# Keys of a cross-attention made as rows and turned, in place of keys made turned with a product for their sums of squares

## The chip, the cores and the metric

The kernel runs on one core of one Trainium2 chip. The metric is the device time of the whole program in microseconds (us). TensorE is PE in the profile (its weight loads PEld), VectorE DVE, ScalarE ACT, GpSimd POOL, and SyncE, which only issues DMAs here, SP. All matrix work that the change touches is in float32; the records show a float32 matmul as two instructions, a transpose as one.

## The reference, cut to what matters

Four batches of 512 tokens (`x`, 512 wide; a context `ctx`, 256 wide) pass through a state-space layer, a quantized feed-forward, a cross-attention and a mixture of experts. The change lies in the cross-attention's keys alone:

```python
k = (ctx @ Wk).reshape(B, Skv, H, D)      # H = 16 heads of D = 128, Skv = 512
k = k * rsqrt(mean(k * k, axis=-1) + 1e-5) * gk
q = q * rsqrt(mean(q * q, axis=-1) + 1e-5) * gq
scores = einsum("bqhd,bkhd->bhqk", q, k) / sqrt(128)
```

For every token and head the kernel needs k with the 128 of a head on the partitions ("turned", times the gain `gk`), and the sum of squares over those 128, which ends as a scale of the softmax's exponent with one value for a token on a partition.

## The kernel before, in words

All instructions of an engine stand in one fixed order, written out by hand for each engine, with semaphores between them. There is no scheduler.

**Units.** The keys are made in 32 *units*, one for each batch and pair of heads (4 x 8; `GH` = 2 heads, `h` = 0, 1). A unit's turned keys go to DRAM (`kt_dram`) and come back in the attention. 18 units (0 to 17) are made in the *first scan*, the state-space layer of batch 0; unit 18 at its end and beyond. After that comes a *turn* for each batch b = 0 to 3: a *front* (the end of that batch's scan, the feed-forward and, in turns 0 to 2, the start of the next batch's scan) and then the attention's eight *groups*, beside which turns 0 to 2 run the next batch's scan. Turns 0 to 2 make two units each, of which the first begins at the end of the turn before; turn 3 has no scan to run and makes eight, seven of them within its front.

**One unit before.** Line numbers are the profile's; every plain matmul has line 1881, the helper `mm`.
- PE, KT(h), `k_turned`: weights are 128 columns of `wk`, 512 tokens stream past, two matmuls. They fill PSUM bank `pp[h]`.
- ACT, `k_out`: for each h a square of the bank into `k_sq` (L962, 128x512) and a copy times the gain into a staging tile (L967). The latter gives the bank back (`pp_drained`).
- PE, SS(h), `k_sums`: four matmuls, each with 128 columns of squares as weights and one column of ones streaming. The sums come out with tokens on partitions, 4 columns in the same bank.
- ACT, `k_sums_out`: mean plus epsilon into `ssv_k` (L975, 128x4).
- SP, `k_dma`: once KT(1) is in PSUM it loads `wk` for the next unit (L541, at times `ctx_att`, L544), then waits until both banks were given back after the gain copies and stores the staging tile (L557).
- POOL, `key_rms`: a power of -1/2 over many units' columns at once (L771).

**What surrounds it.** The first scan has eight rounds. In each, DVE does `times_b` (L1388), the scans (L1396), `times_c` (L1407) and, in rounds 0 to 5, ternary weights (L1355, L1356); ACT makes the decays (L913), weight sums (L935) and moves turned weights (L944 to L955); PE sums the scan's outputs (`y_sum`, weights `arena` or `xc`) and turns weights. Rounds 0 to 5 carry two units each, rounds 6 and 7 one. PE's order within a round is: KT(0), KT(1) of the first unit, y_sum 0, its SS(0), y_sum 1, its SS(1), KT(0), KT(1) of the second unit, weights, its SS(0), weights, its SS(1). SP's order is: the round's `k_dma`s, then the two broadcast loads `bc` of round r + 2 (L536, into `bc` or `xnT`), which DVE's `times_b` of that round waits for, then a staging load of weights (L573, rounds 0 to 3). Units 16 to 18 follow the last y_sum with little beside them, and after them PE starts batch 1's scan.

In a front, DVE works out quantization scales, ACT rounds turned activations (L1052) and makes the gelus (L1056), and PE alternates between transposes and bf16 matmuls.

Of the kernel before, what the change touches and what calls it, by code (L numbers as in the profile page):

```python
# [15 lines left out]
ALU = mybir.AluOpType  # L16
# [73 lines left out]
K_OFF = {"KT": 0, "SS": 2}  # L90
K_HALF = 2
PP_OFF = {"Q": 0, "QT": 2}
# [3 lines left out]
def program(nc, t):  # L96
    ctx = ExitStack()
    with ctx:
# [84 lines left out]
        k_sq_first = dsum  # L183
# [27 lines left out]
        k_sq_turn = qraw.rearrange("p t w -> p (t w)").rearrange("p (h q) -> p h q", h=GH)  # L211
# [134 lines left out]
        k_squares = sem("k_squares")  # L346
# [160 lines left out]
        def _(sp):  # L507
# [224 lines left out]
        def _(pool):  # L732
# [52 lines left out]
            key_rms(G_FIRST * 2, 0, first_columns(0, 2))  # L785
            def turn(b, off, scan):
# [3 lines left out]
                if b == 0:  # L790
                    key_rms(U_FIRST, 0, first_columns(2, 3))
                rstd(2, 3 * b + 2)
                key_rms(units_after(b), b * NG, turn_columns(b))
# [58 lines left out]
        def _(act):  # L852
# [125 lines left out]
            def first_out(n):  # L978
                k_out(n, 0, k_stage_first[n % 2], k_sq_first if n < U_LATE else k_sq_turn)

            def first_sums_out(n, h):
                k_sums_out(*first_unit(n), 0, h)
# [26 lines left out]
            for n in range(U_EARLY):  # L1009
                first_out(n)  # L1010
                for h in range(GH):
                    first_sums_out(n, h)

            for r in range(TC):
# [3 lines left out]
                first_out(units[0])  # L1018
                for i in range(GH):
                    if r + 1 < TC:  # L1020
                        decay(0, r + 1, i)
                    first_sums_out(units[0], i)
                for n in units[1:]:
                    first_out(n)
                if r + 2 < TC:
                    tern(w_out, r + 2, range(0, 2))
                for n in units[1:]:
                    first_sums_out(n, 0)
                if r + 2 < TC:
                    tern(w_out, r + 2, range(2, 4))  # L1030
                for n in units[1:]:
                    first_sums_out(n, 1)
# [3 lines left out]
            for n in range(U_LATE, U_FIRST):  # L1036
                first_out(n)
                for h in range(GH):
                    first_sums_out(n, h)
            for i in range(GH):  # L1040
                act.wait_ge(hc_done[i], TC + 1)
            k_out(unit_at(0, 0)[0], 0, k_stage_turn[0], k_sq_turn)
            k_sums_out(*unit_at(0, 0), 0, 0)

            def turn(b, off, scan):
# [16 lines left out]
                def kt_out(i):  # L1062
# [1471 lines left out]
```

## Time and profile before

| | us |
|---|---|
| median of 3 runs | 2015.83 |
| lowest, highest | 2007.64, 2020.55 |
| profiled execution, its own time | 2035.78 |
| its span | 2033.8 |
| PE busy | 1876.3 (92%) |
| DVE busy | 1392.9 (68%) |
| ACT busy | 1048.6 (52%) |
| POOL busy | 310.4 (15%) |
| mean granted TensorE clock | 0.961 of 2.4 GHz |

The span runs from the first instruction to the last. A busy share is an average over very different stages, and a busy PE is not a PE at its peak: its matmuls overlap, so that the distance from one start to the next, not a record's length, is what an instruction costs. The same holds for ACT, whose short operations start before the one ahead has ended.

### The profile page before, as it was taken

To read this page: it belongs to the slowest core of one execution; us is meant where nothing else is said; L and a number is where in the kernel's file an instruction comes from. 1 tells how busy PE (TensorE), PEld (TensorE's weight loads), DVE (VectorE), ACT (ScalarE), POOL (GpSimd) and SP (SyncE) were. 2 spreads that over 40 slices of the span, in tenths; PEclk is the share of its full clock that TensorE was granted. 3 is DMA by queue.
4 is the path that set the end of the run, shared out by engine and by line. 5 is a ranking of instruction groups with operands and counts; after the bars stand their busy time and mean duration, and the time that the engine had idled before them with its cause. 6 is when DMAs were issued, how large, how long until landed. Compare 5 with 4: busy or idle time off the path is not lost.

```text
span 2033.8 us, 23853 instructions
## 1 busy us (share of the span) xinstructions
PE 1876.3 (92%) x7070; PEld 1073.2 (53%) x7103; DVE 1392.9 (68%) x1775; ACT 1048.6 (52%) x2256; POOL 310.4 (15%) x189
## 2 busy tenths in 40 slices
PE   6799889899999989999999899998899999998895
PEld 2455444556564455656544556564465656543442
DVE  3699726999997689999956999999254232344422
ACT  4667425755554466556536656563445444443430
POOL 1001210211111011212100212120022111114032
PEclk9799989999999989999999899998899999999997
DMA  5256221222222112222221222222224242302333
GB/s 164 80 165 198 83 88 33 68 83 85 85 82 98 39 47 78 85 84 84 79 73 43 73 78 90 75 93 73 78 99 93 64 90 62 88 30 100 125 108 124
DMA packets 115763, 176.23 MB, mean 87 GB/s; under 512 B 12512, under 2 KB 67552, under 8 KB 115184
## 3 DMA queue, kind: packets, MB, share of 16 engines
q1 hardware_dynamic: 101040, 158.58, 24.1%
q0 software_dynamic: 13840, 15.21, 3.7%
q10 hardware_dynamic: 816, 1.57, 0.2%
q8 instruction: 39, 0.64, 0.1%
q14 instruction: 28, 0.23, 0.0%
HBM read 146.76 MB, written 34.87 MB: 89 GB/s over the span
## 4 chain that ended last, share of the span: by engine, by line
PE 64%; issue 16%; DVE 11%; ACT 4%; POOL 2%; another core or an unknown queue 2%; DMA 1%; DVEq 0%; ACTq 0%; SPq 0%; POOLq 0%
PE ps L1881 21%; PE px L1881 14%; PE pp L1881 14%; PE pd L1881 6%; PE po L1881 5%; DVE arena L1396 3%; PE pp L2226 2%; DVE arena L1388 2%; ACT hbuf L1177 1%; ACT arena L913 1%; DVE arena L1407 1%; DVE arena L1414 1%; DVE arena L1374 0%; DVE arena L1372 0%
## 5 line engine op out<-in xcount | busy, mean ns | idle before, releaser
L1396 DVE TENSOR_TENSOR_SCAN arena<-arena 128x512 f32<-128x512 f32 x256 | 294.3, 1205 | 0.6
L762 POOL TENSOR_TENSOR rms<-ssv,minus_half 128x4 f32<-128x4 f32 x64 | 154.3, 2412 | 795.4 <-ACT ssv L1153 795.4
L1177 ACT ACTIVATE hbuf<-ps,shift,rms_k 128x512 f32<-128x512 f32 x256 | 198.5, 777 | 123.5 <-PE ps L1881 116.0
L1881 PE MATMUL ps<-qkT 128*128 128x512 f32 x512 | 256.0, 612 | 5.6 <-ACT hbuf L1177 3.0
L1881 PE MATMUL pp<-wq,xnT 128*128 128x256 f32 x1024 | 233.4, 382 | 2.9 <-issue 1.5
L1881 PEld LDWEIGHTS pp<-wq,xnT 128*128 128x128 f32 x1024 | 192.1, 190 | 40.7 <-issue 13.4
L1598 DVE SCALAR_TENSOR_TENSOR xc<-px,rden,xc 128x512 f32<-128x512 f32 x192 | 136.2, 740 | 85.0 <-PE px L1881 83.4
L1881 PE MATMUL px<-wo,oT 128*128 128x512 f32 x384 | 183.2, 599 | 0.4
L913 ACT ACTIVATE arena<-arena,a_neg 128x512 f32<-128x512 f32 x256 | 163.3, 710 | 14.4 <-DVE arena L1374 8.4
L1881 PEld LDWEIGHTS ps<-qkT 128*128 128x128 f32 x512 | 91.5, 194 | 132.2 <-ACT hbuf L1177 70.5
L1881 PE MATMUL pp<-ctx_att,wk 128*128 128x512 f32 x256 | 136.1, 676 | 22.5 <-ACT ssv_k L975 6.4
L1881 PE MATMUL po<-hbuf,v_sb 128*128 128x512 f32 x256 | 130.7, 592 | 0.0
L1388 DVE TENSOR_TENSOR arena<-arena,bc 128x2048 f32<-128x2048 f32 x56 | 127.8, 2283 | 0.9 <-DVE v_sb L1356 0.6
L1881 PE MATMUL pd<-hbuf,v_sb 128*128 128x512 f32 x256 | 123.0, 603 | 0.0
L1407 DVE TENSOR_TENSOR arena<-arena,bc 128x2048 f32<-128x2048 f32 x52 | 118.8, 2285 | 0.0
L1881 PE MATMUL ps<-wv,ctx_att 128*128 128x256 f32 x512 | 115.8, 379 | 0.0
L1530 DVE SCALAR_TENSOR_TENSOR hbuf<-px,fsc,ws 128x512 f32<-128x512 f32 x64 | 48.0, 751 | 96.1 <-PE px L1881 93.2
L1414 DVE TENSOR_TENSOR arena<-arena 128x2048 f32<-128x2048 f32 x48 | 112.1, 2335 | 2.3
L1612 DVE TENSOR_TENSOR dsum<-dsum,hbuf 128x512 f32<-128x512 f32 x128 | 88.6, 692 | 29.9 <-ACT hbuf L1177 23.6
L1881 PEld LDWEIGHTS ps<-wv,ctx_att 128*128 128x128 f32 x512 | 97.2, 190 | 13.5
L1881 PEld LDWEIGHTS px<-wo,oT 128*128 128x128 f32 x384 | 69.9, 189 | 58.6 <-issue 39.6
L1161 ACT ACTIVATE qk_raw<-pp,rms 128x128 f32<-128x128 f32 x256 | 72.9, 369 | 48.8 <-POOL rms L762 48.6
(324 smaller groups left out, 2901.7 us busy)
## 6 DMA issues: line engine op xcount, KB each, us to landing
bc<-bc_dram SPq DMA_DIRECT2D x56, 512.0 KB, 4.8
wo<-in_Wo SPq DMA_DIRECT2D x32, 512.0 KB, 3.6
wq<-in_Wq SPq DMA_DIRECT2D x32, 512.0 KB, 3.3
qkT<-kt_dram SPq DMA_DIRECT2D x32, 512.0 KB, 3.5
hbuf<-in_w SPq DMA_DIRECT2D x8, 1024.0 KB, 9.5
wk<-in_Wk SPq DMA_DIRECT2D x32, 256.0 KB, 2.8
wv<-in_Wv SPq DMA_DIRECT2D x32, 256.0 KB, 2.8
kt_dram<-xnT SPq DMA_DIRECT2D x14, 512.0 KB, 3.0
```

Of the source, the lines that this page charges most:

```text
L762: nc.gpsimd.tensor_tensor(rms[:, j], ssv[:, j], half, ALU.pow).then_inc(rms_done, 1)
L913: nc.scalar.activation(dA[i][:, e], delta[:, e], ACT.Exp, scale=a_neg[:, e, bass.ds(g * GH + i, 1)]).then_inc(exp_done[i], 1)
L1161: m = nc.scalar.activation(qraw[:, k, h * D:(h + 1) * D], pp[bank][:, i * GW + h * D:i * GW + (h + 1) * D], ACT.Copy, scale=rms[:, j, h, i ...
L1177: nc.scalar.activation(pT[:, h, k], ps[s_use % 2][:], ACT.Exp, bias=shift[:, 0:1], scale=rms_k[:, bass.ds(G * (GH * NT) + (h * NT + k), 1) ...
L1388: V.tensor_tensor(hb[i], du, bc_i[:, 0:1, :].broadcast_to((P, EC, L)), ALU.mult).then_inc(dbu_done[i], 1)
L1396: V.tensor_tensor_scan(hb[i][:, e], dA[i][:, e], hb[i][:, e], 0.0, ALU.mult, ALU.add).then_inc(scan_done[i], 1)
L1407: V.tensor_tensor(dst, hb[i], bc_i[:, 1:2, :].broadcast_to((P, EC, L)), ALU.mult).then_inc(hc_done[i], 1)
L1414: V.tensor_tensor(u, u, hb[i], ALU.add).then_inc(y_added, 1)
L1530: V.scalar_tensor_tensor(hbuf[:, k % 2, j * 512:(j + 1) * 512], bank, fsc[:, 0, 4, k:k + 1], ws1[:, j * 512:(j + 1) * 512], ALU.mult, ALU. ...
L1598: V.scalar_tensor_tensor(xc[:, k], px[bank][:], rden[:, h, k:k + 1], xc[:, k], ALU.mult, ALU.add).then_inc(px_drained[bank], 1)
L1612: V.tensor_tensor(dsum[:, h], dsum[:, h], pT[:, h, k], ALU.add).then_inc(ds_step[h], 1)
L1881: return nc.tensor.matmul(out, lhsT, rhs, start=first, stop=last, **kw)
```

## The change: what it does

- KT(j) becomes **KR(j)** (`k_rows`): weights are 128 tokens of `ctx_att`, the 256 columns of `wk` (both heads) stream past; four matmuls fill bank `pp[j]` with two blocks of tokens as rows.
- ACT (`k_rows_out`) copies each bank to `k_raw` in SBUF (128x512), waits for this own copy (`k_copied`), then squares the bank in place in PSUM in four pieces of 128x128, each with an accumulated row sum that goes straight to `ssv_k`. The last of the four gives the bank back.
- SS(h) becomes **T(h)** (`k_turned`): four PE transposes of `k_raw`, which wait for both copies. ACT then copies the bank times the gain into the staging tile (`k_turned_out`), where the small L975 stood.
- Mean and epsilon move to POOL, one `tensor_scalar` ahead of each power.
- SP waits for T's copies before it stores the staging tile. The code of `k_dma` is the same, but its second wait now stands for a later event.

```diff
-K_OFF = {"KT": 0, "SS": 2}
+K_OFF = {"KR": 0, "KT": 2}
 K_HALF = 2
+K_COUNTED = GH * NT - 2
...
-        k_sq_first = dsum
+        k_raw_first = dsum[:].rearrange("p h q -> p (h q)").rearrange("p (t w) -> p t w", t=NT)
...
             def k_dma(n, G, groups, stage, g_next, ctx_next=None):
 
-                bank, at_ = k_at(n, groups, "KT", 1)
+                bank, at_ = k_at(n, groups, "KR", 1)
                 sp.wait_ge(pp_full[bank], at_)
...
-            def key_rms(end, groups, cols):
-
-                for h in range(GH):
-                    bank, n = k_at(end - 1, groups, "SS", h)
+            def key_rms(call, end, groups, cols):
+
+                pool.wait_ge(k_squared, end * K_COUNTED)
+                for j in range(2):
+                    bank, n = k_at(end - 1, groups, "KR", j)
                     pool.wait_ge(pp_drained[bank], n + 1)
                 dst, src = cols(rms_k), cols(ssv_k)
+                nc.gpsimd.tensor_scalar(src, src, 1.0 / D, EPS, ALU.mult, ALU.add).then_inc(k_mean, 1)
+                pool.wait_ge(k_mean, call + 1)
...
-            def k_out(n, groups, stage, k_sq):
-
-                for h in range(GH):
-                    bank, at_ = k_at(n, groups, "KT", h)
+            def k_rows_out(n, G, groups, k_raw):
+
+                for j in range(2):
+                    bank, at_ = k_at(n, groups, "KR", j)
                     act.wait_ge(pp_full[bank], at_)
-                    nc.scalar.activation(k_sq[:, h], pp[bank][:], ACT.Square).then_inc(k_squares, 1)
-                    if n == 0:
-                        act.wait_ge(gain_step, 3)
-                    if h == 0 and n >= 2:
-                        act.wait_ge(k_stored[n % 2], n // 2 * 16)
-                    nc.scalar.activation(stage[:, h], pp[bank][:], ACT.Copy, scale=kgain[:, 0:1]).then_inc(pp_drained[bank], 1)
-
-            def k_sums_out(n, G, groups, h):
-
+                    nc.scalar.activation(k_raw[:, 2 * j:2 * j + 2].rearrange("p t w -> p (t w)"), pp[bank][:], ACT.Copy).then_inc(k_copied, 1)
+                    act.wait_ge(k_copied, 2 * n + j + 1)
+                    for i in range(2):
+                        for h in range(GH):
+                            rows = pp[bank][:, i * GW + h * D:i * GW + (h + 1) * D]
+                            col = (G * GH + h) * NT + 2 * j + i
+                            m = nc.scalar.activation(rows, rows, ACT.Square, accum_out=ssv_k[:, col:col + 1])
+                            if i == 1 and h == GH - 1:
+                                m.then_inc(pp_drained[bank], 1)
+                            else:
+                                m.then_inc(k_squared, 1)
+
+            def k_turned_out(n, groups, stage, h):
+
+                bank, at_ = k_at(n, groups, "KT", h)
+                act.wait_ge(pp_full[bank], at_)
                 if n == 0:
-                    act.wait_ge(const_set, 4)
-                bank, at_ = k_at(n, groups, "SS", h)
-                act.wait_ge(pp_full[bank], at_)
-                nc.scalar.activation(ssv_k[:, bass.ds(G * (GH * NT) + h * NT, NT)], pp[bank][:, 0:NT], ACT.Identity, bias=eps[:, 0:1],
-                                     scale=1.0 / D).then_inc(pp_drained[bank], 1)
+                    act.wait_ge(gain_step, 3)
+                if h == 0 and n >= 2:
+                    act.wait_ge(k_stored[n % 2], n // 2 * 16)
+                nc.scalar.activation(stage[:, h], pp[bank][:], ACT.Copy, scale=kgain[:, 0:1]).then_inc(pp_drained[bank], 1)
...
-            def k_turned(n, groups, loads, h):
+            def k_rows(n, groups, loads, j):
 
                 pe.wait_ge(ctx_att_in, loads * 16)
                 pe.wait_ge(wk_in, n * 16 + 16)
+                bank, at_ = k_at(n, groups, "KR", j)
+                pe.wait_ge(pp_drained[bank], at_)
+                for i in range(2):
+                    k = 2 * j + i
+                    for c in range(CC):
+                        m = mm(pp[bank][:, i * GW:(i + 1) * GW], ctx_att[:, c, k * P:(k + 1) * P], wk[:, c], c == 0, c == CC - 1)
+                m.then_inc(pp_full[bank], 1)
+
+            def k_turned(n, groups, k_raw, h):
+
                 bank, at_ = k_at(n, groups, "KT", h)
                 pe.wait_ge(pp_drained[bank], at_)
-                for c in range(CC):
-                    m = mm(pp[bank][:], wk[:, c, h * D:(h + 1) * D], ctx_att[:, c], c == 0, c == CC - 1)
-                m.then_inc(pp_full[bank], 1)
-
-            def k_sums(n, groups, k_sq, h):
-
-                bank, at_ = k_at(n, groups, "SS", h)
-                pe.wait_ge(pp_drained[bank], at_)
-                pe.wait_ge(k_squares, n * GH + h + 1)
+                pe.wait_ge(k_copied, n * 2 + 2)
                 for k in range(NT):
-                    m = mm(pp[bank][:, k:k + 1], k_sq[:, h, k * P:(k + 1) * P], ones[:, 0:1], True, True)
+                    m = nc.tensor.transpose(pp[bank][:, k * P:(k + 1) * P], k_raw[:, k, h * D:(h + 1) * D], ident[:])
                 m.then_inc(pp_full[bank], 1)
```

Every call of the old functions is replaced in place: `first_out` by `first_rows_out`, `first_sums` and `kss` by `first_turned` and `ktt`, `kt` by `krr`, and so on. The engines' orders of calls are the same.

ACT in round 3 of the first scan, from the decays on (`arena<-arena,a_neg`). `pp` are the banks, `dsum` holds the squares before and the rows after, `wo` and `wq` are the staging tiles, `ws` and `w2t` receive turned weights. Before:

```order
L913 ACTIVATE arena<-arena,a_neg 128x512 x4
L975 ACTIVATE ssv_k<-pp,eps 128x4
L962 ACTIVATE dsum<-pp 128x512
L967 ACTIVATE wq<-pp,kgain 128x512
L962 ACTIVATE dsum<-pp 128x512
L967 ACTIVATE wq<-pp,kgain 128x512
L946 ACTIVATE ws<-px 128x128
L955 ACTIVATE w2t<-px 128x4x128 x2
L975 ACTIVATE ssv_k<-pp,eps 128x4
L955 ACTIVATE w2t<-px 128x4x128 x2
L975 ACTIVATE ssv_k<-pp,eps 128x4
```

And now:

```order
L919 ACTIVATE arena<-arena,a_neg 128x512 x4
L988 ACTIVATE wo<-pp,kgain 128x512
L968 ACTIVATE dsum<-pp 128x512
L974 ACTIVATE pp,ssv_k<-pp 128x128 x4
L968 ACTIVATE dsum<-pp 128x512
L974 ACTIVATE pp,ssv_k<-pp 128x128 x4
L952 ACTIVATE ws<-px 128x128
L961 ACTIVATE w2t<-px 128x4x128 x2
L988 ACTIVATE wq<-pp,kgain 128x512
L961 ACTIVATE w2t<-px 128x4x128 x2
L988 ACTIVATE wq<-pp,kgain 128x512
```

The staging tile is now written where the small operations stood, the second half of it as the last ACT work of the round.

PE in the same round, y_sum 0's end to the second unit, before:

```order
L1881 MATMUL pd<-xc,ident 128x512
L1881 MATMUL pp<-ones,dsum 128x1 x4
L1881 MATMUL ps<-arena,ident 128x512 x2
L1881 MATMUL po<-arena,ident 128x512
L1881 MATMUL pd<-arena,ident 128x512
L1881 MATMUL pp<-ones,dsum 128x1 x4
L1881 MATMUL pp<-ctx_att,wk 128x512 x4
```

And now:

```order
L1893 MATMUL pd<-xc,ident 128x512
L2000 MATMUL pp<-ident,dsum 128x128 x4
L1893 MATMUL ps<-arena,ident 128x512 x2
L1893 MATMUL po<-arena,ident 128x512
L1893 MATMUL pd<-arena,ident 128x512
L2000 MATMUL pp<-ident,dsum 128x128 x4
L1893 MATMUL pp<-wk,ctx_att 128x256 x8
```

Each four matmuls of one column became four transposes, and four matmuls of 512 columns became eight of 256.

## Rows read from the trace of the kernel before

**Rows 1.** Busy time by stretch: round 4, then stretches named in the text.

```profile
core 0: us, PE busy (x) PEld busy (x) DVE busy (x) ACT busy (x) POOL busy (x), PEclk, DMA share, GB/s
161.00:182.00 21.00, 20.12 (x103) 12.00 (x103) 20.65 (x17) 15.40 (x29) 0.00 (x0) 1.00 0.65 197
245.00:292.00 47.00, 40.14 (x131) 22.46 (x130) 8.07 (x18) 13.20 (x27) 0.95 (x1) 0.82 0.29 97
669.00:743.00 74.00, 70.45 (x301) 36.39 (x305) 48.23 (x82) 39.48 (x46) 3.87 (x2) 0.96 0.14 46
1412.00:1518.00 106.00, 88.35 (x406) 52.57 (x409) 50.33 (x94) 43.38 (x73) 6.27 (x3) 0.92 0.25 92
```

**Rows 2.** Chain that ended last, shares of the span, from the page.

```profile
PE 64%; issue 16%; DVE 11%; ACT 4%; POOL 2%; another core or an unknown queue 2%; DMA 1%; DVEq 0%; ACTq 0%; SPq 0%; POOLq 0%
```

**Rows 3.** Timeline of DVE, rounds 4 to 7: start, length, what, idle before.

```profile
161.50 2.29 DVE L1388 TENSOR_TENSOR arena<-arena,bc 128x2048 f32<-128x2048 f32 x1 [0.21 <-DVE v_sb L1356]
...
182.57 2.29 DVE L1388 TENSOR_TENSOR arena<-arena,xnT 128x2048 f32<-128x2048 f32 x1 [0.21 <-DVE qkT L1356]
...
221.73 2.28 DVE L1388 TENSOR_TENSOR arena<-arena,xnT 128x2048 f32<-128x2048 f32 x1
```

**Rows 4.** Timeline of ACT, a unit and its small operations.

```profile
170.12 0.60 ACT L962 ACTIVATE dsum<-pp 128x512 f32<-128x512 f32 x1 [0.54 <-PE pp L1881]
170.61 0.68 ACT L967 ACTIVATE wq<-pp,kgain 128x512 f32<-128x512 f32 x1
171.18 0.28 ACT L946 ACTIVATE ws<-px 128x128 f32<-128x128 f32 x1
...
174.77 0.26 ACT L975 ACTIVATE ssv_k<-pp,eps 128x4 f32<-128x4 f32 x1 [0.20 <-PE pp L1881]
...
179.37 2.55 ACT L913 ACTIVATE arena<-arena,a_neg 128x512 f32<-128x512 f32 x4
```

**Rows 5.** Chain in order of time: start, length, what.

```profile
402.59 3.45 PE pp L1881 x16
...
1423.80 2.80 DMA wk<-in_Wk
...
1443.15 0.60 ACT dsum L962
...
1450.88 3.43 PE pp L1881 x8
...
1467.61 0.87 PE ps L2074 x8
...
1493.96 0.80 PE pp L1881 x8
```

**Rows 6.** ACT, a query's squares with row sums: timeline, then all 256.

```profile
435.03 0.28 ACT L1148 ACTIVATE qk_raw<-pp 128x128 f32<-128x128 f32 x1 [0.39 <-PE pp L1881]
...
436.20 0.30 ACT L1153 ACTIVATE ssv<-ss,eps 128x4 f32<-128x4 f32 x1
...
L1148 ACT ACTIVATE qk_raw<-pp x256: 254/278/322, 372.4 to 1762.2; 128x128 f32<-128x128 f32 x128
L1148 ACT ACTIVATION_READ_ACCUMULATOR qk_raw<-pp x256: 189/212/257, 372.6 to 1762.3; 128x1 f32 x128
```

**Rows 7.** Issues of SP in round 5; then landings of L536 there.

```profile
213.61 1.30 SPq L536 DMA_DIRECT2D xnT<-bc_dram  x2
...
DMA to landing us min/median/max: 6.6/7.0/7.4
```

**Rows 8.** Issues of SP in rounds 2 and 3; then landings of L536 in 3.

```profile
151.49 1.30 SPq L536 DMA_DIRECT2D bc<-bc_dram  x2
...
171.38 0.36 SPq L557 DMA_DIRECT2D kt_dram<-wq  x1
...
DMA to landing us min/median/max: 6.5/8.0/9.4
```

**Rows 9.** Timeline of POOL, first group of turn 3.

```profile
1513.71 10.52 POOL L771 TENSOR_TENSOR rms_k<-ssv_k,minus_half 128x64 f32<-128x64 f32 x1
```

More of the change, by code:

```diff
@@ L345, in program @@
         k_stored = [sem("k_stored0"), sem("k_stored1")]
-        k_squares = sem("k_squares")
+        k_copied = sem("k_copied")
+        k_squared = sem("k_squared")
+        k_mean = sem("k_mean")
         v_full = [sem("v_full0"), sem("v_full1")]
@@ L984, in ctx_load, with first_turned_out @@
+            def first_turned_out(n, h):
+                k_turned_out(n, 0, k_stage_first[n % 2], h)
             def ctx_load(s):
@@ L1017, in _ @@
                     tern(w_sums, r + 2)
-                first_out(units[0])
+                first_rows_out(units[0])
                 for i in range(GH):
@@ L1021, in _ @@
                         decay(0, r + 1, i)
-                    first_sums_out(units[0], i)
+                    first_turned_out(units[0], i)
                 for n in units[1:]:
-                    first_out(n)
+                    first_rows_out(n)
                 if r + 2 < TC:
@@ L1060, in hq_out, with krr_out, ktt_out @@
                         rounded(("F2T", k), j, hqT[:, k % 2, 4 * j:4 * j + 4, :])
-                def kt_out(i):
-                    k_out(unit_at(b, i)[0], b * NG, k_stage_turn[i % 2], k_sq_turn if scan else k_sq_first)
-                def kss_out(i, h):
-                    k_sums_out(*unit_at(b, i), b * NG, h)
+                def krr_out(i):
+                    k_rows_out(*unit_at(b, i), b * NG, k_raw_turn if scan else k_raw_first)
+                def ktt_out(i, h):
+                    k_turned_out(unit_at(b, i)[0], b * NG, k_stage_turn[i % 2], h)
                 if scan:
                     scan_a(b + 1, turn_, 0)
-                    kss_out(0, 1)
+                    ktt_out(0, 1)
                     scan_a(b + 1, turn_, 1)
-                    kt_out(1)
+                    krr_out(1)
                     scan_silu(b + 1, turn_, range(0, 2))
-                    kss_out(1, 0)
+                    ktt_out(1, 0)
                     scan_silu(b + 1, turn_, range(2, 3))
-                    kss_out(1, 1)
+                    ktt_out(1, 1)
                 else:
-                    kss_out(0, 1)
+                    ktt_out(0, 1)
                     for i in range(1, 4):
-                        kt_out(i)
-                        kss_out(i, 0)
+                        krr_out(i)
+                        ktt_out(i, 0)
                         if i < 3:
-                            kss_out(i, 1)
+                            ktt_out(i, 1)
                 for k in range(NT):
@@ L1113, in turn @@
                 if not scan:
-                    kss_out(6, 0)
-                    kss_out(6, 1)
-                    kt_out(7)
+                    ktt_out(6, 0)
+                    ktt_out(6, 1)
+                    krr_out(7)
                 if scan:
@@ L2022, in _ @@
                 y_sum(r, 0)
-                first_sums(units[0], 0)
+                first_turned(units[0], 0)
                 y_sum(r, 1)
-                first_sums(units[0], 1)
+                first_turned(units[0], 1)
                 for n in units[1:]:
@@ L2039, in _ @@
                 if n > U_LATE:
-                    first_sums(n - 1, 1)
+                    first_turned(n - 1, 1)
                 first_k(n, 1)
-                first_sums(n, 0)
+                first_turned(n, 0)
             n0 = unit_at(0, 0)[0]
-            k_turned(n0, 0, B, 0)
-            first_sums(U_FIRST - 1, 1)
-            k_turned(n0, 0, B, 1)
-            k_sums(n0, 0, k_sq_turn, 0)
+            k_rows(n0, 0, B, 0)
+            first_turned(U_FIRST - 1, 1)
+            k_rows(n0, 0, B, 1)
+            k_turned(n0, 0, k_raw_turn, 0)
             def turn(b, off, scan):
@@ L2101, in ffn1_with_turned, with krr, ktt @@
                     ffn1(k, range(2, 4))
-                def kt(i, h):
-                    k_turned(unit_at(b, i)[0], b * NG, b + B, h)
-                def kss(i, h):
-                    k_sums(unit_at(b, i)[0], b * NG, k_sq_turn if scan or i == 0 else k_sq_first, h)
+                def krr(i, h):
+                    k_rows(unit_at(b, i)[0], b * NG, b + B, h)
+                def ktt(i, h):
+                    k_turned(unit_at(b, i)[0], b * NG, k_raw_turn if scan or i == 0 else k_raw_first, h)
                 for i in range(2):
@@ L2143, in turn @@
                 else:
-                    kss(4, 0)
-                    kt(5, 0)
-                    kss(4, 1)
-                    kt(5, 1)
+                    ktt(4, 0)
+                    krr(5, 0)
+                    ktt(4, 1)
+                    krr(5, 1)
                 ffn1_with_turned(2, 0)
                 if not scan:
-                    kss(5, 0)
+                    ktt(5, 0)
                 ffn2(0, 0, 4)
@@ L2154, in turn @@
                 else:
-                    kss(5, 1)
+                    ktt(5, 1)
                 ffn1_with_turned(3, 1)
                 if not scan:
-                    kt(6, 0)
-                    kt(6, 1)
+                    krr(6, 0)
+                    krr(6, 1)
                 ffn2_with_turned(1)
                 if not scan:
-                    kss(6, 0)
-                    kt(7, 0)
-                    kss(6, 1)
-                    kt(7, 1)
+                    ktt(6, 0)
+                    krr(7, 0)
+                    ktt(6, 1)
+                    krr(7, 1)
                 ffn2_with_turned(2)
                 if not scan:
-                    kss(7, 0)
+                    ktt(7, 0)
                 ffn2(3, 0, 4)
                 if not scan:
-                    kss(7, 1)
+                    ktt(7, 1)
                 def xn_turned():
```

100 lines of the change are left out of this document (49 added, 51 removed).

## The prediction

> **What bounds the kernel now.** I read first the chain that ended last: PE stands for 64% of the span, DVE for 11%, ACT for 4% [rows 2]. So a microsecond of ACT is mostly free and one of PE mostly not. An average decides nothing here, though, and the busy time by stretch [rows 1] shows four different situations for the units:
> - In a round of the first scan DVE is busy 20.65 of 21.00 us, PE 20.12 and ACT 15.40. DVE's rounds start at 161.50 and 182.57, 21.07 apart, with 0.21 idle between, spent on DVE's own previous instruction [rows 3]. DVE sets the pace, PE is just under it, and ACT has some 5.7 us to spare. 16 of the 32 units lie here.
> - In 245 to 292 (units 16 to 18) DVE is busy 8.07 of 47 us and ACT 13.20: PE and its loads are the path.
> - In the front of turn 1 (669 to 743) PE is busy 70.45 of 74 us. The fronts of turns 0 to 2 carry two units each.
> - In the front of turn 3 (1412 to 1518), with seven units, PE is busy 88.35 of 106 us, DVE 50.33, ACT 43.38: a ring in which each waits for the others in turn.
>
> **PE's part.** KT was four matmuls of 512 columns for a unit, each recorded as two: 8 records took 3.43 us [rows 5]. KR is eight of 256 columns, 16 records, and the query's 16 records of that shape took 3.45 us [rows 5]. Same price; the doubled weight loads hide behind columns, as they do for the query. SS(h) was 8 records in 0.80 us; T(h) is four transposes, and 8 transposes took 0.87 us [rows 5], so 0.43. Each of the 64 calls saves 0.37 us, 23.7 us of PE time in all. That is the most that the change could bring by work removed.
>
> **ACT's part.** Before, a unit cost for each h a square of 0.49 us and a copy of 0.57 from start to start (170.12, 170.61, 171.18 [rows 4]) and an L975 of 0.16 (its record is 0.26 long, but the next instruction started 0.16 later, counted from the same overlap as those), together 2.44. Now, for each j: a copy that has to end before the squares start, so its 0.60 record and no overlap, say 0.65; then four squares with row sums. The trace has these, into SBUF: four took from 435.03 to 436.20, where the dependent L1153 started, 1.17 with the end of the last; from start to start I take 0.25 each, 1.0 [rows 6]. Then 0.57 for each gain copy. A unit costs 2 x (0.65 + 1.0) + 2 x 0.57 = 4.44, 2.0 more, 64 us over all units. In place in PSUM no row shows a square. It can hardly cost less than 0.22, and not more than its two records end to end, 0.278 + 0.212 = 0.49 [rows 6]. I take 0.25, the row of the same operation, and keep 0.49 for a rival.
>
> Against the change speaks the fixed part of an instruction, paid eight times instead of twice. The row gives 8 x 0.25 = 2.0 us for what 2 x 0.49 did. The Trainium skill (ScalarE: Activation LUTs, "What ACT_TABLE_LOAD costs") puts an ACTIVATE with immediate operands at 186 ns plus 0.833 a column, with 93 ns of overlap. By that, an estimate, eight pieces cost 1.6 us and ACT's extra would be 1.6 us a unit instead of 2.0. The same page says that writing PSUM is faster for ScalarE than writing SBUF ("Step-by-step: what each stage is for"); no row here shows such a write.
>
> **Where it lands.** *First scan.* ACT gets 2 x 2.0 = 4.0 us more in a round and has 5.7. The decays for the next round, at 179.37 [rows 4], start about 1.2 us later, with some four to spare before DVE's scans, since DVE first has a 2.3 us product after 182.57 [rows 3]. PE gives back 4 x 0.37 = 1.5 us a round. All of this is covered by DVE: worth 0. If the cover went, ACT would set the pace; that is a rival.
>
> But SP is moved. Its store of the staging tile at 171.38 [rows 8] followed the second gain copy at once. Now this copy stands where ACT's last L975 of the round stood, at 174.77 [rows 4], which I estimate to end at 174.6 (PE arrives about 1 us earlier, ACT has 0.6 more per bank, and the copy itself takes 0.6). The store and everything behind it on SP slip by 3.2 us, and right behind it stand the two `bc` loads for DVE's round after next. In round 5 these are issued at 213.61 and the first lands 6.6 later, at 220.2 [rows 7]; DVE needs it at 221.73 [rows 3]. Slack 1.5, slip 3.2: DVE stalls 1.7 us. In round 2 they are issued at 151.49 and land first at about 158.0 by round 3's 6.5 [rows 8], needed at 161.50 [rows 3]: with 3.2 more, just in time. In round 3 they follow the store at 171.38 by less than 1 us and land first near 178.7, needed at 182.57 [rows 3], slack near 4: hidden. I take **+2** for the scan; bounds 0 and, were every one of six rounds 1.5 short, +9.
>
> *Units 15 to 18.* Eight T calls on PE's path save 3.0. Each unit's second KR waits for a 0.6 us gain copy instead of a 0.16 to 0.27 operation, three times +0.4, and T of unit 18 waits 0.65 for the second row copy, with nothing left beside it. **-1**.
>
> *Fronts 0 to 2.* Three T calls each, 1.1 us, less 0.4 for the gain copy that now stands ahead of the rounding of activations: -0.7 each, **-2**.
>
> *Front of turn 3.* The cycle over `wk` is unchanged (2.80 us [rows 5]). After unit 3's second bank ACT needed square, gain copy and L975 before it could round activations; the chain runs through it (1443.15 [rows 5]). Now it is copy, squares and a gain copy, +1.05 us; again, 0.65 each, after units 5 and 6. The T calls give 14 x 0.37 = 5.2, of which I count half where PE is on the path: net **0**. POOL's power of 64 columns took 10.52 us [rows 9] and the group's first use follows on it. The new `tensor_scalar` before it is bounded by 0 and, from the power's fit of 0.16 a column, 10.5; since it is multiply and add, I take 0.7, of which 0.5 is covered by ACT's own work: **+0.2**, with a further microsecond in the range. Its sister calls come where POOL is nearly idle (busy 3.87 of 74 us in a front, 0.00 of 21 in a round [rows 1]): 0.
>
> **Sum:** 2 - 1 - 2 + 0 + 0.2 = -0.8 us against the profiled 2035.78, that is 2035.0. The profiled execution stands 20 us above the median of 2015.83, so the forecast for the median is 2015.0. About 1% (20 us) is what can be told from no change.
>
> **Rivals.**
> 1. *PE's saving comes through.* For it: PE 92% busy, and the chain's 64% [rows 2]. Against: half the T calls lie under DVE's 21.07 us rounds. Outside there are 32, 11.8 us; with none of the ACT delays this is 2004. To pass 1% it needs all 64 or a better granted clock besides (it is 0.82 in 245 to 292 [rows 1]; at most 0.18 x 47 = 8 us are to be had there). That gives 1995. Chance 0.10.
> 2. *ACT becomes the bound of the first scan (slower).* If a square in PSUM costs its full 0.49, a unit costs 2 x (0.65 + 1.96) + 1.14 = 6.4, 3.9 more; a round then holds 15.40 + 7.8 = 23.2 us of ACT work against 21.07. It decides from 0.36 a square on (5.7 us to spare, 16 squares a round). Price: 2.1 x 6 rounds = 13, SP's slip doubled in two rounds 4, three waits of 1 us in turn 3's front plus one in each of units 16 to 18, 6: +23, 2039. For it: the squares are now in the ring between bank and PE; against: the same instruction into SBUF overlaps [rows 6]. Chance 0.12.
> 3. *SP's slip grows.* The 1 MB staging load of weights behind `bc` in rounds 0 to 3 pushes the `wk` load of the next unit, PE comes late to the sums of the scan, and each round loses 1.5 us: +9 to +14, 2027. Seen in DVE waiting for DMA. Chance 0.10, within 1%.
> 4. *It does not do what it says*: KR's weight loads do not hide. SS, which is little but weight loads, takes 0.10 us a record [rows 5]; 8 more in each of 16 units outside the rounds are +13, 2029. The query's row speaks against it [rows 5]. Chance 0.02.
>
> **The numbers.** Forecast within 10 us of 2015: 0.66. The forecast and rivals 3 and 4 are "same", 0.78, less what of rival 3 exceeds 20 us: 0.76. Faster by over 1%: 0.11. Slower by over 1%: rival 2 and a little of what no case names, 0.13. The range from 2001 to 2032 leaves out rival 2, most of rival 1's far end and some of the spread of the runs themselves (13 us between lowest and highest).
>
> **What would show it.** T(h) 8 transposes in 0.87 us; KR 3.45 for 16. Squares in `pp` 0.25 apart and ACT busy about 64 us more, less where records overlap. DVE rounds still 21.07 apart, except that the product that starts round 7 waits for a DMA (1 to 3 us). ACT busy 19 to 20 us of a round. The fronts of turns 0 to 2 shorter by under 1 us, that of turn 3 within 2. Wrong would be it if DVE waits for ACT's decays or PE's sums in the scan, if rounds stretch beyond 21.5, or if a front moves by more than 3 us.

## The result, and the profile after

The changed kernel takes 2032.76 us (median of 4 runs, 2031.59 to 2033.83) beside 2015.6 for the kernel before (4 runs): ratio 1.0088, 95% interval 1.0059 to 1.0117, that is 12 to 24 us slower. Forecast were 2015.0, which is no change that could be told, and a range up to 2032. The median lies 0.8 us above that range.

The two profiled executions, 2035.78 before and 2033.81 after, must not be subtracted. Near the end the one of before has a stall that the other lacks: the timelines of ACT, first of before, then of after, at the same instruction.

```profile
2006.64 0.60 ACT L1265 ACTIVATE oT<-px 128x512 f32<-128x512 f32 x1 [30.18 <-remote]
```

```profile
2004.52 0.60 ACT L1277 ACTIVATE oT<-px 128x512 f32<-128x512 f32 x1 [8.00 <-PE px L1893]
```

It goes with the chip, not with the kernel. The part behind the last turn took 179 to 182 us in the four traces of the runs e5 to e8, all from one chip, and 196 to 204 in the eight of the other runs, from three others, with kernels of both sorts in each group; in the two executions compared here it took 201.8 and 178.6. The kernel before had medians of 2015.6 to 2036.9 on the chips used. So below there are ratios to runs on the same chip, and times of stages within a trace. By stage, from the starts of POOL's marks (L746, L756 and L771 before, L749, L759 and L777 after) that end them:

| Stage | before | after | after, second trace |
|---|---|---|---|
| first scan, to 239.94 before | 239.94 | 259.11 | 260.72 |
| units 16 to 18 | 52.08 | 51.05 | 49.47 |
| front of turn 0 | 90.23 | 92.25 | 92.25 |
| attention of turn 0 | 261.08 | 261.44 | 261.41 |
| front, attention of turn 1 | 117.26, 261.41 | 116.63, 262.92 | 116.63, 262.93 |
| front, attention of turn 2 | 117.40, 277.06 | 119.22, 277.46 | 119.22, 277.45 |
| front of turn 3 | 111.46 | 109.22 | 109.27 |
| attention of turn 3 | 304.13 | 303.93 | 304.41 |

The loss is in the first scan, 19.2 and 20.8 us; the other stages together add 2.0 and 0.9 us (forecast: -2.8). The rounds of DVE in the scan, in the timeline of after (the first line of each):

```profile
119.48 2.29 DVE L1400 TENSOR_TENSOR arena<-arena,bc 128x2048 f32<-128x2048 f32 x1 [0.21 <-DVE v_sb L1368]
...
144.61 2.29 DVE L1400 TENSOR_TENSOR arena<-arena,xnT 128x2048 f32<-128x2048 f32 x1 [2.27 <-DMA xnT<-bc_dram]
...
170.42 2.29 DVE L1400 TENSOR_TENSOR arena<-arena,bc 128x2048 f32<-128x2048 f32 x1 [1.94 <-DMA bc<-bc_dram]
...
195.34 2.29 DVE L1400 TENSOR_TENSOR arena<-arena,xnT 128x2048 f32<-128x2048 f32 x1 [1.94 <-DMA xnT<-bc_dram]
...
221.18 2.29 DVE L1400 TENSOR_TENSOR arena<-arena,bc 128x2048 f32<-128x2048 f32 x1 [1.88 <-DMA bc<-bc_dram]
...
240.89 2.29 DVE L1400 TENSOR_TENSOR arena<-arena,xnT 128x2048 f32<-128x2048 f32 x1 [1.64 <-DMA xnT<-bc_dram]
```

Where they were 21.07 apart [rows 3], they are 25.13, 25.81, 24.92 and 25.84, and DVE waits for `bc`. These four lose 17.3 us; the next, 19.71 for 17.99, loses 1.7. But that wait of 2 us is the end of the story, not its cause. The chain of waits in one round of after:

```profile
146.61 0.86 PE pd L1893 x2
147.46 0.44 PE pp L2000 x4
147.90 4.19 issue
152.09 6.13 PE pp L1893 x16
158.23 0.02 issue
158.25 0.61 ACT dsum L968
158.86 0.02 issue
158.88 1.21 ACT pp L974 x8
...
162.71 3.46 PE pp L1893 x16
```

PE is through with all that it has at 147.90 and stands still for 4.19 us. The profile names nothing for this ("issue"); what starts at 152.09 is KR of the round's second unit, which needs `wk`. SP's issues of after, from the store of one round to the `wk` load of the next, and then how long the `wk` load of 140.19 was under way; then the same of the load of 158.03 before:

```profile
137.62 0.36 SPq L560 DMA_DIRECT2D kt_dram<-wq  x1
138.02 1.31 SPq L539 DMA_DIRECT2D xnT<-bc_dram  x2
139.38 0.51 SPq L576 DMA_DIRECT2D hbuf<-in_w  x1
140.19 1.48 SPq L544 DMA_DIRECT2D wk<-in_Wk  x1
...
163.77 0.36 SPq L560 DMA_DIRECT2D kt_dram<-wq  x1
164.17 1.31 SPq L539 DMA_DIRECT2D bc<-bc_dram  x2
165.52 0.51 SPq L576 DMA_DIRECT2D hbuf<-in_w  x1
166.19 1.57 SPq L544 DMA_DIRECT2D wk<-in_Wk  x1
...
DMA to landing us min/median/max: 11.8/11.8/11.8
```

```profile
158.03 0.37 SPq L541 DMA_DIRECT2D wk<-in_Wk  x1
...
DMA to landing us min/median/max: 7.7/7.7/7.7
```

140.19 + 11.8 is 152.0, to 0.1 us when PE goes on. With nothing ahead of it this load takes 2.8 us. Before, 6.5 us lay between `bc` (151.49 [rows 8]) and the `wk` load behind it (158.03); now 2.2 (138.02 to 140.19): the 1 MB of `bc` and the 1 MB staging load have moved back with the store, `wk` of the next unit has not. It is released by the keys of the next round's first unit, which PE had done at 140.16 (136.44, 3.72 long).

And the delay closes a ring, from one issue of `wk` to the next, by two paths of nearly the same length. By SP: landing 11.8, KR 6.1, ACT, the transposes and the gain copy up to the store 5.6, `bc` and staging load on SP 2.4, together 25.9 us. By PE: landing 11.8, KR 6.1, sign matmuls and transposes, with a wait for ACT between, 4.3, KR of the next round's first unit 3.6, together 25.8. The issues are 26.0 apart (140.19, 166.19). SP was through with the staging load at 166.03; the keys it waits for were complete at 166.17 (the last line of the chain above). So the path by PE ended last, by 0.1 us.

The granted clock adds to it. Busy times of after in the two stretches:

```profile
core 0: us, PE busy (x) PEld busy (x) DVE busy (x) ACT busy (x) POOL busy (x), PEclk, DMA share, GB/s
147.80:152.00 4.20, 0.10 (x1) 0.00 (x0) 4.20 (x5) 1.14 (x2) 0.00 (x0) 0.78 0.72 288
152.09:158.20 6.11, 6.11 (x18) 4.93 (x19) 6.08 (x5) 1.81 (x9) 0.00 (x0) 0.60 0.04 15
```

The DMA engines move 288 GB/s while PE waits, 15 GB/s after. The granted clock is 0.60 of full speed over the 6 us right behind PE's idle time, most of them thus at 1.2 of its two levels 1.2 and 2.4 GHz, and the 16 records of KR take 6.12 us there, 3.62 where PE had not waited: 2.5 us more. The four waits took 4.92, 4.19, 4.08 and 3.72 us, the four KRs behind them 1.7, 2.5, 1.5 and 2.9 more than 3.62.

The rest of the profile after. ACT's timeline in a unit, the squares' group, and a group of transposes:

```profile
139.30 0.62 ACT L968 ACTIVATE dsum<-pp 128x512 f32<-128x512 f32 x1
139.96 0.26 ACT L974 ACTIVATE pp<-pp 128x128 f32<-128x128 f32 x1
140.13 0.19 ACT L974 ACTIVATION_READ_ACCUMULATOR pp<-pp 128x1 f32 x1
140.22 0.27 ACT L974 ACTIVATE pp<-pp 128x128 f32<-128x128 f32 x1
...
141.07 0.58 ACT L968 ACTIVATE dsum<-pp 128x512 f32<-128x512 f32 x1
...
L974 ACT ACTIVATE pp<-pp x256: 260/265/271, 72.3 to 1523.6; 128x128 f32<-128x128 f32 x128
L974 ACT ACTIVATION_READ_ACCUMULATOR pp<-pp x256: 182/186/196, 72.5 to 1523.8; 128x1 f32 x128
L2000 PE MATMUL pp<-ident,dsum x184: 272/273/421, 74.2 to 1531.3; 128*128 128x128 f32 x184
```

A copy with its wait 0.66, four squares from 139.96 to 141.07, 0.28 each [rows 4, 6]. POOL's new operation, and the power [rows 9]:

```profile
1535.09 0.24 POOL L774 TENSOR_SCALAR ssv_k<-ssv_k 128x64 f32<-128x64 f32 x1
1535.42 10.52 POOL L777 TENSOR_TENSOR rms_k<-ssv_k,minus_half 128x64 f32<-128x64 f32 x1
```

### The profile page after: what moved, and what is told of

Same layout as the page of the kernel before. It is cut to its first block, busy times and chain, and to the rows that moved or that the text cites. A ratio compares the mean times of both kernels' runs of the same rounds, so it can differ in the third digit from the quotient of the medians.

```text
span 2031.8 us, 24337 instructions
## 1 busy us (share of the span) xinstructions
PE 1860.1 (92%) x7070; PEld 1095.2 (54%) x7103; DVE 1392.6 (69%) x1775; ACT 1109.9 (55%) x2704; POOL 313.2 (15%) x195
## 4 chain that ended last, share of the span: by engine, by line
PE 68%; issue 20%; ACT 5%; DVE 5%; POOL 2%; DMA 1%; SPq 0%; ACTq 0%; DVEq 0%; POOLq 0%
PE ps L1893 22%; PE pp L1893 15%; PE px L1893 14%; PE pd L1893 7%; PE po L1893 6%; PE pp L2240 1%; ACT hbuf L1189 1%; ACT arena L919 1%; ACT pp L974 1%; PE pp L2000 1%; DVE arena L1426 1%; DVE ln_st L1429 0%; POOL ln_r L759 0%; DVE xc L1610 0%; POOL rms_k L777 0%
## 5 line engine op out<-in xcount | busy, mean ns | idle before, releaser
L1893 PE MATMUL pp<-wk,ctx_att 128*128 128x256 f32 x512 | 138.1, 427 | 41.0 <-issue 21.8
L1893 PEld LDWEIGHTS pp<-wk,ctx_att 128*128 128x128 f32 x512 | 107.4, 216 | 63.8 <-issue 43.9
```

The source lines that it names most:

```text
L1893: return nc.tensor.matmul(out, lhsT, rhs, start=first, stop=last, **kw)
```

## The experiments

Theory A: the slip of SP's store puts `bc` and staging load right ahead of the next unit's `wk` load, PE waits for `wk`, and the ring becomes slower than DVE. Theory B: ACT's additional work between KR and the transposes stretches the rounds.

**The slip undone (e1_store_last).** In the changed kernel:

```
-                for n in round_units(r):
-                    first_dma(n)
-                (bc loads, staging load)
+                for n in units:
+                    first_dma(n, loads if n == units[-1] else None)
     (k_dma: wk load, then loads() if given, then the wait for the gain copies, then the store)
```

> The changed kernel; in the first scan SP issues the bc loads and the weight staging load before it waits for the round's last gain copy and stores the key tile, so these loads stand again about 1.3 us behind the wk load, as before the change. Nothing else moves. Theory A (SP's order: the wk load of the next unit stands behind 1 MB of bc and 1 MB of staging load, lands 12 us after its issue and holds PE, ACT and again SP): rounds of DVE go back from 25.1 to 25.8 us to 21.0 to 21.5, the scan is 17 to 20 us shorter, median 2014 (2009 to 2018). Theory B (ACT's 2 us more for each unit, between KR and the transposes, stretch the ring): rounds stay at 24 to 26, median 2028 to 2033.

Measured: ratio 0.9982 (0.9968 to 0.9997). DVE's rounds are 21.06, 21.07, 21.07, 21.17 and 17.99 long, the scan ends at 240.14. ACT does all of its additional work in it. A holds; B, as the cause of the loss, falls. Where the ring is slower than DVE, ACT's squares do lie in it (the 1.21 us of the chain above); at DVE's pace they cost the scan nothing.

**The slip alone in the kernel before (e2_before_slip).**

```
-                    bank, at_ = k_at(n, groups, "KT", h)
+                    bank, at_ = k_at(n, groups, "SS", h)     # first scan only
                     sp.wait_ge(pp_drained[bank], at_ + 1)
```

> The kernel before; only SP's store of a unit's key tile in the first scan waits for the L975s of the unit too, so that the store and all behind it are issued some 3 us later, as in the changed kernel. PE and ACT do what they did. Theory A: the slip alone is enough, rounds of 24 to 26 us where there were 21.07, 12 to 19 us longer, median 2030 (2026 to 2035). Theory B: without ACT's extra work the slip costs only what DVE waits for bc in round 7, 1.7 us: 2015 to 2019.

Measured: 1.0087 (1.0058 to 1.0116), the changed kernel's own ratio. Rounds of 24.82, 24.07, 25.81, 25.04 and 22.01 us. From DVE's round 1 to the end of the scan it takes 19.4 us more than before; the changed kernel 19.1 and, in its second trace, 20.5. Neither PE nor ACT does anything new here: one wait on SP is enough for the whole loss. PE waits 2.64 to 3.57 us four times, with KT at 5.06 to 6.52 us behind it for 3.68. SP was through with the staging load at 134.99 and issued `wk` at 135.92, when PE had done KT of the first unit (132.21, 3.68 long): the ring by PE alone.

**A smaller staging load (e3_small_stage, e10_half_stage).**

```
-                    w_stage(r + 4, r % 2, 2)
+                    w_stage_part(r + 4, r % 2)     # columns 0:256 (e3), 0:1024 (e10)
```

> The changed kernel; in rounds 0 to 3 of the first scan the staging load brings 256 of the 2048 columns (128 KB of 1 MB), so that the quantized weights of the last part are made of old columns. Theory A: 0.9 MB less stands ahead of the wk load, which lands 3 to 5 us earlier; PE no longer waits (3.7 to 4.9 us in each of four rounds) and its keys run at the full clock; rounds 0 to 3 shrink to 21 to 23 us, 10 to 16 us in all, median 2020 (2016 to 2025). Theory B: no change, 2031 to 2034.

> The changed kernel; in rounds 0 to 3 the staging load brings 1024 of the 2048 columns (512 KB of 1 MB), the others stay old. At the 197 GB/s of a round, 0.5 MB are 2.7 us. The changed kernel's ring is 25 to 26 us; less 2.7, and less the 2.5 us that KR loses at the lower granted clock if PE waits less, 20 to 23 us: about DVE's 21.07. So most of the loss is gone with half of the bytes, ratio 0.998 to 1.003. Were the loss in proportion to the bytes, half of it: 1.003 to 1.006.

Measured: with 128 KB 0.9997 (0.9976 to 1.0017), better than the 2020 expected: rounds of 21.07, `wk` lands after 7.5 to 8.0 us. In round 7 DVE waits 1.05 us for `bc`, all that is left of the slip. With 512 KB 1.0038 (1.0023 to 1.0052), outside the 0.998 to 1.003 expected and within what was named for a loss in proportion to the bytes: the rounds take 22.21, 23.03 and 23.70, `wk` lands after 9.4 to 11.1. The ring's 25.9 minus 2.7 us is 23.2, about what they reach; that is still over DVE's 21.07, and each of the three rounds pays the difference. PE on e10, at KR behind its wait:

```profile
144.46 5.24 PE L1897 MATMUL pp<-wk,ctx_att 128*128 128x256 f32 x16 [2.55 <-issue]
```

Two of its four waits, 2.55 and 2.38 us, still have KR at the lower clock behind them (5.24 and 5.38); behind those of 3.23 and 1.77 it takes 3.69.

**The loads between the units (e4_loads_between).**

```
+                first_dma(units[0])
+                loads()                  # bc and staging load
+                for n in units[1:]: first_dma(n)
```

> The changed kernel; in the first scan the bc loads and the staging load are issued between the two units of a round, some 10 us earlier than in the kernel before, and stand ahead of the wk load for the next round's first unit in place of its second. Theory A: DVE never waits for bc; rounds 21.0 to 21.5, median 2012 to 2016, unless the wk load for the first unit becomes late in turn (issued after KR of the second unit, needed about 8 us later, 12 us if it lands as late as now): then 1 to 4 us for each of four rounds, 2018 to 2028. Theory B: 2028 to 2033.

Measured: 1.0216 (1.0189 to 1.0242), the worst of all. The rounds are 26.31, 30.19, 28.23, 30.20 and 24.46 us. The 8 us of slack that I expected aren't there: behind KR of the second unit PE has only two groups of sign matmuls and a few transposes before KR of the next round's first unit, some 4 us, and now that unit's `wk` had the 2 MB ahead of it. PE stands still for 7.55, 8.12, 7.11, 8.24 and 6.25 us; the second and the last of these end with the context's load, which is issued behind `wk`:

```profile
194.12 8.24 issue
202.37 6.10 PE pp L1897 x16
```

The second unit's `wk` has the sums of the scan to hide behind, 8 us. So of the places tried for the whole 2 MB on SP's queue only one costs nothing: right behind the `wk` load for a round's first unit, where the kernel before has it.

**The staging load on ScalarE's queue (e5_stage_act).**

```
-                    sp.wait_ge(stage_used[r % 2], r // 2 + 2)      # SP
-                    w_stage(r + 4, r % 2, 2)
+                    act.wait_ge(stage_used[r % 2], r // 2 + 2)     # ACT, end of its round
+                    act.dma_start(stage[r % 2]..., src).then_inc(stage_in[r % 2], 16)
```

> The changed kernel; the staging load of rounds 0 to 3 is issued from ScalarE's queue at the end of ScalarE's round, no longer from SP's. The bytes are the same, only they don't stand in SP's queue ahead of the wk load. If the order in one queue is what delays wk (theory A1), this is worth what leaving the bytes out was: wk lands after 8 us at most, rounds of 21.07, ratio to the kernel before 0.997 to 1.002. If the 16 DMA engines themselves are the limit (theory A2), wk's packets share with the 1 MB all the same and land 10 to 12 us after issue: rounds of 24 to 26, ratio 1.005 to 1.009.

Measured: 0.9969 (0.9955 to 0.9983), the best ratio of a kernel that leaves nothing out. `wk` lands after 8.2 to 9.7 us, the rounds are 21.8, then 21.06. But ACT issued the load at 129.24, 1.4 us ahead of `bc` (130.65), where SP would have issued it 1.4 behind: the run mixes another queue with a head start, and so does not tell A1 from A2. The Trainium skill (DMA: Bandwidth & Descriptors, "Issuing engines are not separate DMA queues") says that all queues run on the same 16 DMA engines and that starting DMAs from several engines only saves the time of issuing. No run here measures the throughput that this is about.

The next run keeps the queue and changes the order alone.

**The staging load behind `wk` (e11_stage_behind_wk).** Same queue, same bytes:

```
-  store, bc, staging load | wk (next round's k_dma)
+  store, bc | wk, staging load
```

> The changed kernel; SP issues the staging load of a round directly behind the next wk load (that of the second unit) in place of directly ahead of it, some 1 to 2 us later than now. Same bytes, same queue, store and bc where the change has put them. In e5_stage_act the load was also issued 2.7 us earlier than by SP, so that run does not separate the order from the head start; this one does. If what counts is what stands ahead of wk: wk lands 8 to 9 us after issue, rounds of 21.07 to 21.8, scan 17 to 19 us shorter, ratio 0.996 to 1.001. If the engines carry all that is under way side by side, wk lands 11 to 12 us after issue as now: ratio 1.006 to 1.010.

Measured: 1.0007 (0.9996 to 1.0019). SP and PE in it:

```profile
135.02 0.37 SPq L544 DMA_DIRECT2D wk<-in_Wk  x1
135.43 1.86 SPq L578 DMA_DIRECT2D hbuf<-in_w  x1
```

```profile
144.38 3.69 PE L1896 MATMUL pp<-wk,ctx_att 128*128 128x256 f32 x16 [1.05 <-issue]
```

The store and `bc` slip as in the changed kernel, the load is even issued later, and the loss is gone: `wk` lands after 9.3 us (8.9 to 9.4 in the four rounds), PE waits 1.05 and KR takes 3.69. The rounds are 21.06 to 21.19, and only round 7 waits for `bc`, 1.20 us.

What is issued behind `wk` is not free either. In the next round of this trace there is no staging load, `wk` (197.97) is issued 2.2 us after `bc` (195.73), 2.0 in the rounds with one, and it lands after 6.9 us. So, by these rows, the 1 MB costs `wk` 2.4 us when issued 0.4 us behind it and 4.9 when issued ahead of it (11.8 in the changed kernel).

**What ACT's squares cost (e6_one_square, e7_squares_sbuf).** Both from e1_store_last:

```
-                    for i in range(2):
-                        for h in range(GH):
+                    for i in range(1, 2):                  # e6: the last square of four
+                        for h in range(GH - 1, GH):
```

```
-   activation(k_raw[...], pp[bank], ACT.Copy).then_inc(k_copied, 1)
+   activation(k_raw[...], pp[bank], ACT.Copy).then_inc(pp_drained[bank], 1)      # e7
-   activation(rows, rows, ACT.Square, accum_out=...)       # rows in pp
+   activation(k_junk[...], rows, ACT.Square, accum_out=...) # rows in k_raw
```

> The version that stores last (e1_store_last), with one square of 128 columns for each row bank in place of four: six of eight squares with row sums of each unit are left out (the sums of the other rows are a constant). ACT loses 1.7 us a unit. In the scan nothing may change (DVE sets its pace). If ACT's squares lie on the path outside the scan as the prediction counted them (0.4 for a wait in units 16 to 18 and in fronts 0 to 2, 1.05 + 2 x 0.65 in the front of turn 3): 3 to 7 us less than e1_store_last, ratio 0.995 to 0.997. If they are covered everywhere: the same as it, 0.998.

> The version that stores last, with the squares read from the SBUF copy of the rows and written to SBUF of their own: the copy alone frees the PSUM bank, and the transposes wait for the two copies, not for the squares. ACT does as much. If the squares between copy and freed bank cost time outside the scan: 1 to 4 us less than e1_store_last, ratio 0.996 to 0.9975. If not, 0.998 as e1_store_last.

Measured: e6 0.9964 (0.9951 to 0.9976), e7 0.9978 (0.9967 to 0.9988), beside 0.9982 for e1. Six of eight squares left out in 32 units are worth some 4 us at most, and the intervals overlap; taking the squares out of the bank's way is worth nothing that can be told. The front of turn 3 took 110.69 us in e6 and 112.50 in e7, at a granted clock of 0.94, and 109.18 in e1, at 0.97. The changed kernel's own code took 112.03 at 0.94 in e5 (see the fronts below), so the 2 to 3 us expected can't be read from this stage.

**Controls.** The kernel before with e1's order:

> The kernel before with SP's order of e1_store_last (loads ahead of the wait for the round's last gain copy and the store). Control: whether e1_store_last's small gain over the kernel before comes from the order. In the kernel before the store waited only 0.9 us, so the loads move by about 1 us: ratio 0.999 to 1.001. If the order itself brought the gain: 0.998.

Measured 0.9997 (0.9984 to 1.0010): the order brings nothing of its own. All three edits together:

> Three of the edits together: stores last (e1_store_last), the staging load on ScalarE's queue (e5_stage_act), squares from the SBUF copy (e7_squares_sbuf). The scan is already at DVE's pace in each of them, so they should not add up: ratio 0.996 to 0.998. If each gain were of its own, 0.993 to 0.995.

Measured 0.9983 (0.9975 to 0.9992): they do not add up. The changed kernel again:

> The changed kernel once more, beside the others on one chip. Ratio 1.006 to 1.012 as measured. Its second trace tells which stage differences come back: the scan 19 us longer, units 16 to 18 and the front of turn 3 shorter by 1 and 2 us, the front of turn 2 longer by 2 us. What does not come back within 0.5 us is the spread of one execution.

Measured 1.0090 (1.0070 to 1.0110); its stages stand in the table above. From the turns on they come back within 0.5 us. The scan does not, 1.6 us longer, and units 16 to 18 are 1.6 shorter; both together end at 310.16 and 310.19. That the turns come back does not make their differences the kernel's: e5, with the same code in them, has other fronts (see below).

So the change with SP's order mended is 0.2 to 0.3% faster than the kernel before (e1, e5, e7, e9: 0.9969 to 0.9983, each interval below 1), 3 to 6 us. e11, in which PE still waits 0.6 to 1.6 us a round, isn't (1.0007).

## Why the prediction was wrong

**The step that failed is the scan's term, +2 us with bounds 0 and +9.** It measured 19.2. The slip itself was right: forecast 3.2, measured 3.4 (the first round's store went from 107.75 to 111.15). What I then asked was only who needs `bc` and when. That answer was nearly right too: DVE stalls in round 7 for 1.7 us by the forecast, for 1.05, 1.50 and 1.20 us in e3, e5 and e11, where PE is not held up. I did not ask, in the sum, what comes behind the moved loads on the same queue.

**Rival 3 had the mechanism, and its price was 1.5 us a round.** The four rounds lost 3.8 to 4.8 (3.0 to 5.3 in the second trace). Two things were left out. First the slack: before, the `wk` load of 158.03 landed at 165.7, and PE began the KT that needs it at 166.40. There was 0.7 us of slack, and 1.5 to 3.2 in the other three rounds, readable beforehand:

```profile
165.59 0.95 PE L1881 MATMUL pp<-ones,dsum 128*128 128x1 f32 x8
166.40 3.68 PE L1881 MATMUL pp<-ctx_att,wk 128*128 128x512 f32 x8
```

Then the landing went from 5.2 to 7.7 us up to 11.3 to 12.7, since loads issued 4.5 to 6.8 us closer ahead of it were still under way. Second the ring: what is late for PE is late for the next KR, which releases the next `wk` load, and for ACT and the store, and so for the loads that made it late. Such a delay is not paid once and then hidden again under DVE; with the lower clock behind each wait the ring ran at 26 us against DVE's 21.07, and every round paid. Seen in DVE waiting for DMA it was, as the rival said, but the larger wait stood on PE, unnamed.

**Right.** KR costs what KT did at the full clock (3.46 for 16 in the chain), and T takes 0.44 for four where I said 0.43 [rows 5]. The copy 0.66 for 0.65; POOL's tensor_scalar 0.24, within the 0.7 (the one in the scan took 2.42, where POOL had nothing else to do). ACT's busy time rose by some 61 us for 64.

**Squares.** They are 0.28 apart where I took 0.25, so a unit costs 2 x (0.66 + 1.11) + 1.14 = 4.68 for 4.44. Rival 2 needed 0.36 and did not come; e1 shows ACT's load covered. Eight squares take 2.2 us by this. The estimate of 1.6 was worked out from the Trainium skill (ScalarE: Activation LUTs, "What ACT_TABLE_LOAD costs"), by which 128 columns come to 0.20 us apart. These are 0.28 apart, with a read of the accumulator (0.186 us of record) behind every square (0.265), and the measurement decides. A smaller slip: units 0 and 1 are made ahead of the rounds, so that the rounds hold 14 units and not 16; no term of the sum turns on it.

**Units 16 to 18, fronts.** Forecast -1 for units 16 to 18; measured -1.0 and -2.6. For the fronts, forecast -0.7 three times and 0; measured +2.0, -0.6, +1.8 and -2.2. The forecast left the granted clock of these stages out, and they differ more with it than by the change. Rows of the fronts of turns 0, 2 and 3, before and after:

```profile
292.02:382.25 90.23, 80.59 (x348) 43.94 (x352) 65.51 (x100) 51.14 (x82) 14.57 (x7) 0.96 0.14 47
...
1022.00:1139.40 117.40, 105.25 (x417) 57.02 (x421) 80.61 (x125) 59.01 (x96) 11.17 (x6) 0.93 0.17 57
...
1416.46:1527.92 111.46, 95.03 (x435) 58.50 (x440) 48.57 (x90) 47.39 (x95) 15.54 (x7) 0.92 0.25 89
```

```profile
310.16:402.41 92.25, 83.99 (x339) 45.27 (x343) 65.29 (x99) 52.00 (x83) 14.78 (x6) 0.91 0.14 45
...
1043.40:1162.62 119.22, 106.63 (x414) 58.91 (x419) 80.61 (x125) 62.19 (x124) 11.26 (x8) 0.91 0.16 56
...
1440.08:1549.30 109.22, 86.57 (x435) 60.77 (x440) 48.59 (x90) 61.81 (x193) 15.80 (x7) 0.97 0.25 90
```

Some of the experiments run the changed kernel's code in these stages at another granted clock. First the front of turn 0 in e11, then those of turns 2 and 3 in e5:

```profile
289.77:379.13 89.36, 79.61 (x339) 42.72 (x343) 65.31 (x99) 51.71 (x83) 14.77 (x6) 0.96 0.13 46
```

```profile
1019.98:1136.36 116.38, 103.57 (x414) 57.38 (x418) 80.58 (x125) 61.89 (x124) 11.44 (x8) 0.93 0.16 57
1414.08:1526.11 112.03, 89.66 (x435) 62.96 (x440) 48.58 (x90) 61.92 (x193) 15.79 (x7) 0.94 0.24 86
```

At the same granted clock the fronts are 0.9 us shorter in turn 0 (0.96), 0.6 in turn 1 and 1.0 in turn 2 (both 0.93; for turn 1 by the table), near the forecast's 0.7. In turn 3 the same code takes 109.22 at 0.97 and 112.03 at 0.94, beside 111.46 at 0.92 before. So the +2.0 and the +1.8 go with the granted clock and not with the change, and most of the -2.2 does; no trace has both kernels at one granted clock in turn 3's front. The kernel before moves in the same way: its front of turn 0 took 93.13 at 0.91 in e8. Why one trace is granted more of the full clock in a stage than another stays open.

**Rival 1** (PE's saving comes through) had the right sign for what is left when the order is mended: 3 to 6 us of its 20. **Rival 4** is excluded by KR's 3.46.

## What to carry to other kernels

When an edit moves a wait on a queue that issues loads, follow every load behind it to its consumer, and not only the load that comes first. For each compare landing with the consumer's start in the trace; here one with 0.7 us of slack stood three issues behind the store. If that consumer's result releases the same queue again, work out the period of that ring and compare it with the present pace, since what it lacks is paid in every round. Bulk loads belong behind the small load that an engine stands on: exchanging `wk` and the staging load was worth 0.8% here. And compare a stage between two traces only at the same granted clock: here the same code took 2.8 us more or less in one front.

## What the runs showed of the hardware

- A 256 KB load landed 2.7 to 3.3 us after its issue with nothing close ahead of it, 5.6 to 7.3 when issued 2.0 to 2.7 us behind 1 MB (after, e3, e5, e10, e11, in the rounds without a staging load), 7.5 to 8.0 behind 1.1 MB (e3), 8.9 to 9.4 behind 1 MB with another 1 MB issued right behind it (e11), 9.4 to 11.1 behind 1.5 MB (e10) and 11.3 to 12.9 behind 2 MB (both traces of after). The engines moved 288 GB/s meanwhile (147.80 to 152.00).
- Behind idle time of PE of 3.7 to 5.1 us the 16 records of KR took 5.1 to 6.6 us (both traces of after), behind 0.3 to 1.9 us 3.69 (e5, e10, e11). In between both came: 5.24 and 5.38 behind 2.55 and 2.38 us, but 3.69 behind 3.23 (e10). In the kernel before, one KT took 5.40 us behind two short waits of 0.87 and 0.29 us (132.32).
- A wait for a DMA can stand as "issue" on PE; it was found by adding the landing time to the issue on SP.
